# A graph and mixture-of-experts network: VectorE's sum and one-hots are moved ahead of the block's own messages

## The chip, the cores and the metric

One core of a Trainium2 chip runs the whole kernel. The metric is the time of one execution in microseconds; the kernel before took 3406.29 us, the median of three runs (3405.17 to 3412.83).

## The reference, cut to what matters

Four layers are added one after the other to x (128 tiles of 128 nodes, 128 features each): a graph layer with a dense adjacency, a mixture of 4 experts that is gated by a graph attention over 524,288 edges, a dense graph attention, and a mixture of 8 experts. The change lies in the edges' attention of the second layer:

```python
a_src = (h * att_src).sum(-1)
a_dst = (h * att_dst).sum(-1)
e = jax.nn.leaky_relu(a_src[src] + a_dst[dst], negative_slope=0.2)
e_max = jax.ops.segment_max(e, dst, num_segments=M)
ee = jnp.exp(e - e_max[dst])
denom = jax.ops.segment_sum(ee, dst, num_segments=M)
alpha = ee / (denom[dst] + 1e-16)
msg = h[src] * alpha[:, :, None]
agg = jax.ops.segment_sum(msg, dst, num_segments=M).reshape(M, HEADS * NUM_EXPERTS) + b_gat
```

## The kernel before, in words

The kernel is several programs behind each other. The first ones sort the edges by destination, compute the first layer and build a table of the nodes. The last program, `layers`, holds the edges' attention, the experts and the dense attention, interleaved by hand. Edges are taken in 128 blocks, one for each 128 destination nodes; a block has nine chunks of 128 edges (`GC` is 9, padding included).

For a block b these steps follow each other across the engines:

- SyncE loads the block's window of sorted destinations, broadcast over all partitions (`window`, L1670), which waits for `oh_ready` of the block two before; further row and hub windows are queued behind it. GpSimd gathers the source nodes' rows, nine indirect DMAs a block (L1750), into a ring of four; it waits for `msg_ready` of the block that held the slot, and for counts of the experts' matmuls.
- VectorE (DVE) makes two one-hots (`hots`, L2083 and L2086): which edge goes to which node, for the sum, and its transpose, for the look-up. It signals `oh_ready`.
- TensorE (PE) looks up the destination's part of the score for each edge (`look_up`, L1762, nine matmuls) and signals `look_done`.
- DVE makes the messages (`messages`, L1084 to L1091, six operations that wait for each other) once `look_done` and `gathered` allow, and signals `msg_ready`.
- PE sums the messages by destination (`attend`, L1771, nine matmuls into one bank) and signals `sum_done`; right behind it, it does the look-up of block b + 1.
- DVE adds the sum to its accumulator (`add_sum`, L1095 and L1097) in the attend of block b + 1.

One-hots, messages and PSUM banks are doubled: block b uses number b % 2.

The order of the work is written out by hand: each engine goes through turns `i`, and a turn has four attends (blocks 4i + 2 to 4i + 5), called first to fourth here. Between them stand the steps of the experts of a group of four tiles and of the dense attention of two later stages. On PE, an expert is an up-projection (L1786, a record of four matmuls) and a down-projection (L1795, sixteen). On DVE, `expert` adds its result to x (L2181). Behind the second attend DVE adds biases, makes norms (L2206 to L2220) and the scaled x of L2216, for which PE waits at L1879 (`turn_x2`). ScalarE (ACT) does the GELUs (L1940), copies out of PSUM (L1957 the turned gates, L1999 the projection h) and counts (L2028). Its copy at L1999 is what DVE waits for at L2228.

In the first turns (i < 1) DVE also makes one-hots of the remaining edges (L2107), which PE counts (L1815), and in the turns before i = 4 there are no experts of the last layer yet.

Of the kernel before, what the change touches and what calls it, by code (L numbers as in the profile page):

```python
# [31 lines left out]
GC = 9  # L32
GROUP = GC * P
RING = 4
# [1040 lines left out]
def high_halves(split):  # L1075

    return split.bitcast(BF16).rearrange("p c a (f t) -> p c a f t", t=2)[:, :, :, :, 1]


def messages(v, me, looked, got, look, split):  # L1080

    high = high_halves(split)
    msg, left, last = (split[:, :, a, :] for a in range(PARTS))
    me.link(v.tensor_reduce(look[:, :, :], looked.rearrange("p (c a h) -> p c h a", c=GC, a=PARTS), AX.X, ALU.add))  # L1084
    me.link(v.tensor_tensor(look[:, :, :], look[:, :, :], got[:, :, HC + HEADS:TAB], ALU.mult))
    me.link(v.tensor_tensor(msg[:, :, HC:ROW], look[:, :, :], got[:, :, HC:HC + HEADS], ALU.max))
    me.link(v.tensor_tensor(msg[:, :, 0:HC].rearrange("p c (h f) -> p c h f", f=CH),  # L1087
                            got[:, :, 0:HC].rearrange("p c (h f) -> p c h f", f=CH),
                            over(msg[:, :, HC:ROW].unsqueeze(3), [P, GC, HEADS, CH]), ALU.mult))
    me.link(v.tensor_tensor(left, msg, high[:, :, 0, :], ALU.subtract))  # L1090
    return v.tensor_tensor(last, left, high[:, :, 1, :], ALU.subtract)  # L1091
# [403 lines left out]
def layers(nc, adj, sorted_src, sorted_dst, rest_sums, first, table, made, w, keep, out):  # L1495
# [20 lines left out]
    LOOK = PARTS * HEADS  # L1516
# [7 lines left out]
    with Scope(nc, "lay") as s:  # L1524
        ident, iota_b, node_no, least, base_no = (keep[n] for n in ("ident", "iota_b", "node_no", "least", "base_no"))
        idx, to, wide, hub_wide = (keep[n] for n in ("idx", "to", "wide", "hub_wide"))
        node_col, halves, got = (keep[n] for n in ("node_col", "halves", "got"))
# [8 lines left out]
        look = s.sb("look", [P, GC, HEADS])  # L1536
        split = s.sb("split", [P, 2, GC, PARTS, ROW])
# [50 lines left out]
        b_att = [s.bank(f"b_att{k}") for k in range(2)]  # L1588
# [7 lines left out]
        wide_in, hub_in, rows_in, gathered = (keep[n] for n in ("wide_in", "hub_windows_in", "rows_in", "gathered"))  # L1596
# [3 lines left out]
        look_done = s.sem("look_done")  # L1600
        msg_ready = s.sem("msg_ready")
# [54 lines left out]
        def has_block(b):  # L1656
            return 0 <= b < tiles
# [408 lines left out]
        def _(v):  # L2066
            edge, pick, dense, add = (Done(v, sem) for sem in own)
# [14 lines left out]
            def hots(b):  # L2082
                v.tensor_tensor(oh[:, b % 2, :, :], node_col[:, :, :], over(low[:, b, :].unsqueeze(1), [P, P, GC]),  # L2083
                                ALU.is_equal)
                v.wait_ge(wide_in[b % 2], 16 * (b // 2) + 16)
                v.tensor_scalar(oht[:, b % 2, :], wide[:, b % 2, :], node_no[:, b:b + 1], None, ALU.is_equal)\  # L2086
                    .then_inc(oh_ready, 1)

            def attend(b):
                if has_block(b):  # L2090
                    v.wait_ge(look_done, b + 1)
                    v.wait_ge(gathered[b % RING], (16 * GC) * (b // RING + 1))
                    messages(v, edge, b_att[b % 2][:, 0:GC * LOOK], got[:, b % RING, :, :], look,
                             split[:, b % 2, :, :, :]).then_inc(msg_ready, 1)
                if has_block(b - 1):
                    v.wait_ge(sum_done, b)
                    edge.mark(add_sum(v, edge, b_att[(b - 1) % 2][:, GC * LOOK:GC * LOOK + SUM], added,
                                      acc[:, b - 1:b, :]))
                if b >= 0 and has_block(b + 1):
                    hots(b + 1)  # L2100

            def rest_hots_of(n):

# [186 lines left out]
            for i in range(-1, LAST):  # L2290
                b, m, t, f = 4 * i + 2, i - QUAD, i - QUAD - 1, i - QUAD - 2
# [147 lines left out]
```

## Time and profile before

| what | value |
|---|---|
| median of three runs | 3406.29 us |
| the profiled execution's own time | 3408.03 us |
| its span | 3406.0 us |
| PE busy | 75% of the span |
| DVE busy | 72% |
| ACT busy | 52% |
| GpSimd (POOL) busy | 34% |
| mean granted clock of PE | 0.867 of full speed |

The span is the time from the first to the last instruction on the core; the execution's own time has some 2 us around it. A matmul's record has a modelled end. The granted clock of PE has two levels, 1.00 (2.4 GHz) and 0.50 (1.2 GHz). Idle time is shown in brackets behind an instruction, with what ended it, as far as the profile could tell; "issue" and "remote" stand where no instruction could be named.

### The profile page before, as it was taken

What the parts mean: (1) busy time and instruction counts of PE and PEld (TensorE: products, weight loads), DVE (VectorE), ACT (ScalarE), POOL (GpSimd) and SP (SyncE); (2) the same over time, 40 slices, a digit from 0 to 9 for tenths busy, and PEclk for the clock granted to TensorE, in tenths of its full rate; (3) what the DMA queues carried; (4) which work ended last, traced back from release to release, by engine and by line L of the source; (5) the groups of instructions that cost most, each with busy time, mean ns of one, the idle gap of its engine ahead of it and who ended that gap; (6) DMA issues with size and microseconds to landing.
All of it is one profiled execution on the core that took longest, in us unless ns stands there. A gap on an engine that the chain in (4) does not pass through costs nothing.

```text
span 3406.0 us, 48930 instructions
## 1 busy us (share of the span) xinstructions
PE 2558.5 (75%) x15405; PEld 1894.7 (56%) x15406; DVE 2451.7 (72%) x7195; ACT 1765.8 (52%) x3180; POOL 1157.5 (34%) x1205
## 2 busy tenths in 40 slices
PE   1789888988888832115878788788888888788889
PEld 0566666666656622014656565556656656556666
DVE  7888888878778645237667776876777777686774
ACT  0566666666666612014555555555455555555654
POOL 0000000000000027655656555555655656556200
PEclk9999999999999965556888888888888888888899
DMA  2011111111111033223232332323323232232300
GB/s 91 32 50 50 47 53 44 53 41 38 50 38 44 32 100 86 38 55 89 63 84 66 71 87 62 85 70 78 76 63 92 66 85 66 62 93 66 82 13 10
DMA packets 228554, 210.48 MB, mean 62 GB/s; under 512 B 70780, under 2 KB 160584, under 8 KB 227656
## 3 DMA queue, kind: packets, MB, share of 16 engines
q1 hardware_dynamic: 190152, 190.84, 18.8%
q0 software_dynamic: 37280, 14.38, 4.7%
q8 instruction: 123, 2.02, 0.2%
q10 hardware_dynamic: 864, 2.14, 0.2%
q14 instruction: 135, 1.11, 0.1%
HBM read 159.49 MB, written 47.74 MB: 61 GB/s over the span
## 4 chain that ended last, share of the span: by engine, by line
DVE 22%; PE 19%; another core or an unknown queue 9%; issue 9%; ACT 2%; POOL 2%; DVEq 0%; DMA 0%; ACTq 0%; POOLq 0%
PE lay_b_y L1795 8%; PE lay_b_z L1786 7%; DVE keep_x L2181 6%; POOL keep_got L1750 2%; PE lay_b_b L1837 1%; DVE lay_oht L2086 1%; PE lay_b_att L1762 1%; DVE lay_split L1090 1%; DVE lay_oh L2083 1%; DVE lay_split L1091 1%; DVE lay_stats L2206 1%; PE lay_b_g L1887 1%; DVE lay_split L1087 1%; ACT lay_unused L2028 1%
## 5 line engine op out<-in xcount | busy, mean ns | idle before, releaser
L1750 POOL DMA_INDIRECT keep_got<-node_table,keep_idx x1143 | 1122.1, 982 | 772.5 <-issue 304.9
L1795 PEld LDWEIGHTS lay_b_y<-lay_w,lay_hid 128*128 128x128 f32 x4096 | 542.2, 206 | 164.5 <-issue 162.6
L1786 PE MATMUL lay_b_z<-lay_xin,lay_w 128*128 128x512 f32 x1024 | 581.3, 696 | 11.6 <-ACT lay_hid L1940 7.7
L1795 PE MATMUL lay_b_y<-lay_w,lay_hid 128*128 128x128 f32 x4096 | 551.9, 290 | 38.5 <-issue 34.9
L2181 DVE SCALAR_TENSOR_TENSOR keep_x<-lay_b_y,lay_gates,keep_x 128x128 f32<-128x128 f32 x1024 | 288.0, 344 | 373.4 <-remote 204.4
L1940 ACT ACTIVATE lay_hid<-lay_b_z,lay_b 128x512 f32<-128x512 f32 x512 | 330.3, 682 | 405.6 <-PE lay_b_z L1786 207.1
L899 POOL MEMSET find_ones<- 128x128 f32 x1 | 0.2, 204 | 1203.5 <-POOLq L49 1203.5
L2028 ACT ACTIVATE lay_unused<-keep_hub_wide,keep_halves 128x1152 bf16<-128x1152 uint16 x256 | 320.3, 1251 | 138.1 <-DMA keep_hub_wide<-sorted_dst 68.5
L1786 PEld LDWEIGHTS lay_b_z<-lay_xin,lay_w 128*128 128x128 f32 x1024 | 201.1, 218 | 176.8 <-issue 154.2
L472 PE MATMUL front_b_h<-front_xt,front_m 128*128 128x512 f32 x512 | 256.8, 628 | 41.1 <-ACT front_act_m L582 33.8
L225 DVE TENSOR_TENSOR sort_keys<-sort_keys 128x1024 f32<-128x1024 f32 (+2 forms) x182 | 257.5, 1415 | 32.1 <-ACT sort_keys L550 29.1
L226 DVE TENSOR_TENSOR sort_keys<-sort_keys 128x1024 f32<-128x1024 f32 (+2 forms) x182 | 256.9, 1412 | 0.0
L428 PE MATMUL front_b_h<-front_w,front_agg_t 128*128 128x512 f32 x256 | 140.1, 674 | 94.2 <-DVE front_hb L716 71.9
L1771 PE MATMUL lay_b_att<-lay_split,lay_oh 128*128 128x60 bf16 x1152 | 90.9, 229 | 158.5 <-DVE lay_split L1091 112.2
L582 ACT ACTIVATE front_act_m<-front_b_h,front_mb 128x512 f32<-128x512 f32 x256 | 170.3, 684 | 64.9 <-PE front_b_h L472 64.5
L491 PEld LDWEIGHTS front_b_turn<-front_m,front_act_m 128*128 128x128 f32 x1536 | 184.2, 192 | 31.1 <-issue 31.1
L491 PE MATMUL front_b_turn<-front_m,front_act_m 128*128 128x128 f32 x1536 | 187.0, 275 | 0.0
L1771 PEld LDWEIGHTS lay_b_att<-lay_split,lay_oh 128*128 128x128 bf16 x1152 | 84.2, 156 | 176.7 <-DVE lay_split L1091 122.3
L472 PEld LDWEIGHTS front_b_h<-front_xt,front_m 128*128 128x128 f32 x512 | 89.0, 195 | 156.4 <-ACT front_act_m L582 100.4
L437 PE MATMUL front_b_ht<-front_diag,front_hb 128*128 128x128 f32 x1024 | 131.6, 282 | 35.0 <-ACT front_diag L573 22.7
L437 PEld LDWEIGHTS front_b_ht<-front_diag,front_hb 128*128 128x128 f32 x1024 | 120.5, 193 | 47.5 <-issue 29.2
L2181 DVE SCALAR_TENSOR_TENSOR keep_x<-lay_y,lay_gates,keep_x 128x128 f32<-128x128 f32 x512 | 145.7, 346 | 0.7
(397 smaller groups left out, 4244.0 us busy)
## 6 DMA issues: line engine op xcount, KB each, us to landing
keep_wide<-sorted_dst SPq DMA_DIRECT2D x128, 288.0 KB
keep_hub_wide<-sorted_dst SPq DMA_DIRECT2D x128, 288.0 KB
made<-front_y SPq DMA_DIRECT2D x128, 256.0 KB, 2.0
lay_y<-made SPq DMA_DIRECT2D x32, 1024.0 KB
keep_got<-node_table,keep_idx POOLq DMA_INDIRECT x1152
front_adj<-in_adj SPq DMA_DIRECT2D x32, 256.0 KB, 3.1
keep_x<-in_x SPq DMA_DIRECT2D x32, 256.0 KB, 3.5
lay_adj<-in_adj SPq DMA_DIRECT2D x32, 256.0 KB
```

The lines of the kernel that those rows point to most:

```text
L225: me.mark(v.tensor_tensor(o[:, :, 0, :], s[:, :, 0, :], s[:, :, 1, :], ALU.min))
L226: return v.tensor_tensor(o[:, :, 1, :], s[:, :, 0, :], s[:, :, 1, :], ALU.max)
L437: mm = pe.matmul(b_ht[c % 2][:, P * j:P * j + P], hb[:, j, P * c:P * c + P], diag[:, j, :], start=True, stop=True)
L472: pe.matmul(b_h[c][:, :], m1[:, e, P * c:P * c + P], flat(xt[:, :, :]), start=True, stop=True)\
L491: mm = pe.matmul(bank[:, P * j:P * j + P], act_m[n % 2][:, c, P * j:P * j + P], m2[:, e * MK + c, :], start=(c == 0), stop=(c == MK - 1))
L1750: pool.indirect_dma_start(out=got[:, b % RING, c, :], out_offset=None, in_=table, in_offset=bass.IndirectOffsetOnAxis(ap=idx[:, b % AHEAD, ...
L1771: mm = pe.matmul(b_att[b % 2][:, GC * LOOK:GC * LOOK + SUM], oh[:, b % 2, :, c], high_halves(split[:, b % 2, :, :, :])[:, c, :, :] .rearra ...
L1786: pe.matmul(b_z[c][:, :], w1[:, e, P * c:P * c + P], flat(xin[g % 2][:, :, :]), start=True, stop=True).then_inc(z_done, 1)
L1795: mm = pe.matmul(b_y[n % 2][:, P * j:P * j + P], hid[n % 2][:, c, P * j:P * j + P], w2[:, e * HK + c, :], start=(c == 0), stop=(c == HK - 1))
L1940: act.activation(hid[n % 2][:, c, :], b_z[c][:, :], ACT.Gelu, bias=b1[:, e * HK + c:e * HK + c + 1]).then_inc(hid_ready, 1)
L2028: act.activation(unused[:, :], hub_wide[:, b % 2, :], ACT.Sign, bias=halves[:, u, b:b + 1], accum_out=signs[:, u, b:b + 1]).then_inc(count ...
L2181: ins = v.scalar_tensor_tensor(out=here, in0=made_here[:, P * j:P * j + P], scalar=gates[n][:, g * TB + j, e:e + 1], in1=here, op0=ALU.mul ...
```

## The change

In DVE's `attend(b)` of the last program, the adding of block b - 1's sum and the one-hots of block b + 1 are put ahead of block b's messages. PE's, GpSimd's, SyncE's and ACT's orders stay.

```diff
             def attend(b):
-                if has_block(b):
-                    v.wait_ge(look_done, b + 1)
-                    v.wait_ge(gathered[b % RING], (16 * GC) * (b // RING + 1))
-                    messages(v, edge, b_att[b % 2][:, 0:GC * LOOK], got[:, b % RING, :, :], look,
-                             split[:, b % 2, :, :, :]).then_inc(msg_ready, 1)
                 if has_block(b - 1):
                     v.wait_ge(sum_done, b)
                     edge.mark(add_sum(v, edge, b_att[(b - 1) % 2][:, GC * LOOK:GC * LOOK + SUM], added,
                                       acc[:, b - 1:b, :]))
                 if b >= 0 and has_block(b + 1):
                     hots(b + 1)
+                if has_block(b):
+                    v.wait_ge(look_done, b + 1)
+                    v.wait_ge(gathered[b % RING], (16 * GC) * (b // RING + 1))
+                    messages(v, edge, b_att[b % 2][:, 0:GC * LOOK], got[:, b % RING, :, :], look,
+                             split[:, b % 2, :, :, :]).then_inc(msg_ready, 1)
```

## Rows read from the trace of the kernel before

**Rows 1.** Windows: stretch, its us, busy us (count) of PE, PEld, DVE, ACT, POOL, PEclk.

```profile
1290.00:1612.00 322.00, 84.73 (x666) 66.41 (x666) 164.01 (x493) 73.54 (x129) 207.45 (x202) 0.52 0.31 69
1612.00:3220.00 1608.00, 1310.41 (x7830) 963.55 (x7831) 1173.98 (x4269) 877.90 (x1517) 917.43 (x945) 0.86 0.32 75
```

**Rows 2.** Timeline of one first attend: start us, us, engine, line, operation, idle before.

```profile
2433.76 0.27 DVE L1084 TENSOR_REDUCE lay_look<-lay_b_att 128x36 f32<-128x108 f32 x1
...
2435.25 0.35 DVE L1091 TENSOR_TENSOR lay_split<-lay_split 128x180 f32<-128x180 f32 x1
...
2435.65 0.75 PE L1771 MATMUL lay_b_att<-lay_split,lay_oh 128*128 128x60 bf16 x9 [1.04 <-DVE lay_split L1091]
...
2436.64 0.51 DVE L2086 TENSOR_SCALAR lay_oht<-keep_wide,keep_node_no 128x1152 bf16<-128x1152 uint16 x1
...
2437.21 0.71 PE L1762 MATMUL lay_b_att<-keep_far_parts,lay_oht 128*128 128x12 bf16 x9 [0.81 <-DVE lay_oht L2086]
```

**Rows 3.** Waits of the steady part, 1612 to 3220: total us, times, longest.

```profile
PE lay_b_att L1762 <- DVE lay_oht L2086: 20.3, 25, 0.8
...
PE lay_b_att L1762 <- issue: 18.0, 25, 1.2
```

**Rows 4.** Timeline behind the second attend of that turn, and L1879 of another turn.

```profile
2446.74 0.51 DVE L2086 TENSOR_SCALAR lay_oht<-keep_wide,keep_node_no 128x1152 bf16<-128x1152 uint16 x1
...
2447.31 0.70 PE L1762 MATMUL lay_b_att<-keep_far_parts,lay_oht 128*128 128x12 bf16 x9 [0.38 <-issue]
...
2447.88 1.96 PE L1786 MATMUL lay_b_z<-lay_xin,lay_w 128*128 128x512 f32 x4
...
2451.46 0.60 PE L1829 MATMUL lay_b_b<-keep_ident,lay_gates 128*8 128x128 f32 x4
...
2452.99 0.59 ACT L1957 ACTIVATE lay_gate_t<-lay_b_b 8x512 f32<-8x512 f32 x1 [1.90 <-PE lay_b_b L1829]
...
2453.99 1.11 DVE L2216 TENSOR_SCALAR lay_xn<-keep_x,lay_mv,lay_rstd 128x128 f32<-128x128 f32 x4
...
2455.16 0.66 PE L1879 MATMUL lay_b_g<-keep_ident,lay_xn 128*128 128x128 f32 x4 [1.38 <-issue]
...
2994.43 0.66 PE L1879 MATMUL lay_b_g<-keep_ident,lay_xn 128*128 128x128 f32 x4 [0.57 <-DVE lay_xn L2216]
```

**Rows 5.** Timeline of the third attend of the same turn.

```profile
2460.22 0.52 DVE L2086 TENSOR_SCALAR lay_oht<-keep_wide,keep_node_no 128x1152 bf16<-128x1152 uint16 x1
...
2462.62 0.67 PE L1771 MATMUL lay_b_att<-lay_split,lay_oh 128*128 128x60 bf16 x9
...
2463.13 0.68 PE L1762 MATMUL lay_b_att<-keep_far_parts,lay_oht 128*128 128x12 bf16 x9
```

**Rows 6.** Timeline of DVE at the start of the last program: its waits.

```profile
1366.71 0.27 DVE L1084 TENSOR_REDUCE lay_look<-lay_b_att 128x36 f32<-128x108 f32 x1 [4.86 <-DMA keep_got<-node_table,keep_idx]
...
1436.69 0.27 DVE L1084 TENSOR_REDUCE lay_look<-lay_b_att 128x36 f32<-128x108 f32 x1 [10.37 <-remote]
...
1490.19 0.27 DVE L1084 TENSOR_REDUCE lay_look<-lay_b_att 128x36 f32<-128x108 f32 x1 [16.51 <-issue]
...
1529.32 0.69 DVE L2228 TENSOR_TENSOR lay_lg<-lay_h,lay_a 128x512 f32<-128x512 f32 x1 [10.76 <-issue]
...
1548.19 0.27 DVE L1084 TENSOR_REDUCE lay_look<-lay_b_att 128x36 f32<-128x108 f32 x1 [5.89 <-issue]
```

**Rows 7.** PE by windows of 8 us from L1879 (busy, PEclk), and an up-projection.

```profile
1671.50:1679.50 8.00, 6.71 (x44) 1.00 0.37 84
1734.50:1742.50 8.00, 7.46 (x39) 0.79 0.37 84
...
2439.85 3.78 PE L1786 MATMUL lay_b_z<-lay_xin,lay_w 128*128 128x512 f32 x4
```

**Rows 8.** Timeline of a gather behind its wait, and of a window load's issue.

```profile
2435.86 0.94 POOL L1750 DMA_INDIRECT keep_got<-node_table,keep_idx  x1 [1.70 <-DVE lay_split L1091]
...
2447.41 0.33 SPq L1670 DMA_DIRECT2D keep_wide<-sorted_dst  x1
```

## The prediction, made before the changed kernel was run

> **What bounds the kernel now.** I read the windows of the stages first, then the timeline of one turn of the last program, then DVE's waits at its start. The last program has a slow start of 322 us in which PE is busy 84.7 us, and a steady part of 1608 us in which PE is busy 1310 and DVE 1174 [rows 1]. In the steady part neither is the bound alone: each turn (four blocks, eight experts; 1608 us over 27 turns, 59.6 us) hands the work to and fro. Only these two stretches hold an `attend`, so nothing before 1290 us and after 3220 us can change, apart from its place in time.
>
> One attend of DVE runs from 2433.76 to 2437.15: the messages to 2435.60 (1.84 us), then sum and one-hots to 2437.15 (1.55 us). PE starts its sum matmuls 0.05 us after the messages end, waits again, and starts the look-up 0.06 us after the one-hots end; it is through at 2437.92 [rows 2]. The list of waits counts 50 such waits ahead of the look-up in the steady part, 38.3 us in all, so 0.77 each [rows 3]: in about half of its 108 attends PE is early, in the others DVE is.
>
> **The change part by part.** It adds, removes and resizes no instruction: six message operations, two of the sum and two of the one-hots stay, 3.39 us an attend. What moves is the signal `msg_ready`, 1.55 us later behind a start of DVE that waits for nothing, and `oh_ready`, 1.84 us earlier.
>
> *PE at an attend where it is early.* It now waits once, for the messages, which end where the one-hots ended (2437.15). Then sum and look-up follow each other: the look-up starts 0.51 us behind the sum's start in an attend without a wait [rows 5]. It ends at 2437.15 + 0.06 + 0.51 + 0.71 = 2438.43, against 2437.92: **0.51 us later**. That is so 50 times [rows 3], in the first and second attend of a turn. What takes it up: in the first attend, PE's wait for the same DVE in the second one. In the second, the wait at L1879 for `x2_ready`. DVE goes from the end of its one-hots (2447.25) to L2216 (2455.10) on its own, and PE had waited 1.38 us there [rows 4]. L1879 stands with such a wait in all 26 turns whose windows I compared; 1.38 is the usual value, the smallest is 0.57, in a turn where PE came late to its attends and so loses nothing. So 50 x 0.51 = 25.5 us of delay are shown and I put **0** of them on the path; if that cover were gone, the second attend alone would cost 27 x 0.51 = 13.8 us.
>
> *Third and fourth attends.* DVE's one-hots end at 2460.74 and PE begins its sum at 2462.62, without idle time [rows 5]. The messages now end at 2460.74: still 1.88 us ahead. Cost 0; if PE were as early as in the first attends, 0.51 each.
>
> *Start of the last program.* Here DVE waits ahead of the messages: 4.86 us for the gathered rows (the last of five such waits, at 1366.71), then 10.37, 16.51 and 5.89 us, and another of their kind at 1515, between the last two [rows 6]. The one-hots and the sum now lie inside these waits. From the end of such a wait to the end of the attend DVE takes 1.84 instead of 3.39, and is 1.55 us ahead. PE's look-up, which the next wait hangs on, begins 1.84 + 0.06 + 0.51 = 2.41 behind the wait's end instead of 3.45: 1.04 ahead. The five waits for gathers are paced by GpSimd, so only the last one's gain goes on: 1.0. Of the four long waits I count 1.04 each for those at 1436.69 and 1490.19 and 1.55 for that at 1548.19 (PE comes late there, and the 0.51 is not added); the one at 1515 is followed by a wait of 10.76 us at L2228 for ScalarE, which takes its gain. Sum 1.0 + 1.04 + 1.04 + 1.55 = **4.6 us gained**. Bounds: 0, if what ends those waits isn't moved by PE's earlier look-up; 9 x 1.55 = 14 us if all nine count in full. I take 4.6, nearest to what the order of the rows lets through.
>
> *Queues.* GpSimd waits for `msg_ready` of the block four back (1.70 us ahead of the gather at 2435.86) [rows 8]; it starts up to 1.55 us later. The rows it fetches are used by the attend four blocks on, a turn of 59.6 us later, so 0. In the start its five blocks of gathers have no wait for DVE. Were that ring the bound, it would be 1.55 a block. SyncE issues its window load 0.16 us after the one-hots end (2447.41) [rows 8]; it may issue 1.84 us sooner, with its next row and hub loads behind it: more lead for loads that nobody waits for in the steady part, 0. DVE's wait for `sum_done` now stands at the head of the attend; PE made that sum an attend before (through at 2436.40 [rows 2], while the next attend of DVE ends at 2447.25 and so begins near 2443.9), so 0; behind it are queued only the one-hots and messages that waited there anyway.
>
> *The clock.* PE's up-projection of four matmul records took 3.78 us at the granted clock of 1.2 GHz and 1.96 at 2.4 [rows 7, 4]. In 9 of the 26 stretches of 8 us from L1879 on, the granted clock was 0.79 on average, as in the stretch at 1734.5, and in the others 1.00, as at 1671.5: 0.21 x 8 / 0.5 makes 3.4 us at 1.2 GHz, which follow the wait of 1.38 us there and cost PE 1.7 us of work. The change shortens exactly this wait, to some 0.87 us, and lengthens those at the first two attends. I enter 0, and keep 9 x 1.7 = 15 us of gain for the range.
>
> **Sum.** 0 + 0 - 4.6 + 0 = -4.6 us. The profiled execution took 3408.03 us (span 3406.0), 1.7 above the median of 3406.29, so it would come to 3403.4, and the median to **3401.7 us**. A measurement of this kernel tells 0.2% (6.8 us) from no change.
>
> **Rivals.**
> 1. *PE's clock stays up behind L1879.* For: each drop of the kind counted above follows that idle time [rows 7], and half or more of nine could vanish at 1.7 us each: 7.7 more, 3394 us. Against: the same idle time appears at the attends. Chance 0.28.
> 2. *Slower: the cover at L1879 isn't real.* Place: L1879, once a turn. Price 0.51 x 27 = 13.8, less 4.6: +9.2, 3415.5 us. It decides where PE's true slack is under 0.51 us. For it: ScalarE begins to copy the turned gates at 2452.99, 0.93 us after PE's record of them ended (2451.46 + 0.60) [rows 4], though it had been idle 1.90 us: PE may run behind its records. Against: 1.38 - 0.93 leaves 0.45, just below 0.51, so at most a tenth of a us a turn would pass by that row. The Trainium skill, Perfetto Trace Analysis, Tensor Engine Instruction, says that the profiler estimates a matmul's end and doesn't observe it. By that rule, the row's 0.93 us is what the record leaves out. Chance 0.12.
> 3. *Slower: the clock falls at the second attend.* PE's idle pieces there (0.38 us at 2447.31 [rows 4], 0.77 in the mean) become a single one ahead of the sum. If PE ran at 1.2 GHz for 3.4 us behind it, it would lose 1.7 us, of which 0.87 are covered: 0.8 a turn, 22 us if in all 27, about 3424; with a third of the turns 3409. Against: the up-projection behind that attend (2447.88) took 1.96 us, at full clock. The Trainium skill, TensorE: Matmul & The Clock Gate, Part 1, says that idling throttles the array and activity releases it. By that rule, a longer single pause is worse than two short ones, and the sum would be +3 to +18 in place of -4.6. The trace agrees only at L1879. Chance 0.06.
> 4. *It changes nothing that lasts.* The long waits at the start end when they did before, and all later waits take the rest: 3406.3 us. For: the three long ones shown have a releaser that the view calls "issue" or "remote", not a named instruction [rows 6]. Chance 0.12.
>
> **How the numbers follow.** Forecast 0.42 (3401.7; its own range 3396 to 3406, as the start's gain runs from 0 to 10). Faster by over 0.2% is under 3399.5: rival 1 whole, and a third of the forecast's case: 0.28 + 0.14 = 0.42. Slower is over 3413.1: rival 2 and most of 3, 0.12 + 0.04 = 0.16. The rest, 0.42, is within 0.2%. The range goes down to rival 1 with most of its nine drops gone (3401.7 - 14 = 3388) and up to rival 2 (3415).
>
> **What would show it.** PE's wait ahead of L1762 gone in the first attends, that ahead of L1771 there near 2.6 us instead of 1.04; the wait at L1879 near 0.87; the long waits of DVE now ahead of the same L1084 with L2083 and L2086 inside them; turns of the same length; the last program's first 320 us shorter by 4 to 5. Wrong, if L1879 keeps a wait of 0.87 and the turns still lengthen (then it is GpSimd, the loads or the clock), if L1879's wait falls by more than 0.51, or if the granted clock of the steady part moves from 0.86 by over 0.01.

## The result, and the profile after

The changed kernel took **3418.88 us** (median of 15 runs, 3407.47 to 3428.32); the kernel before took 3401.59 us beside it (15 runs, 3389.99 to 3412.83). The ratio is **1.0054, 95% interval 1.0039 to 1.0069**: slower by 0.54%, 17.3 us between the medians and 18.4 by the ratio. Forecast was 3401.7 us, with a range up to 3415. It started from a median of 3406.29 us of three runs, so as a ratio it was 0.9986.

The profiled execution of the changed kernel has a span of 3412.0 us against 3406.0 before, so the two traces show 6 us of the 17. The window of the last program's steady part, changed kernel (columns as in [rows 1]):

```profile
1612.00:3220.00 1608.00, 1298.78 (x7777) 951.61 (x7778) 1164.17 (x4243) 871.87 (x1511) 918.70 (x941) 0.85 0.31 73
```

Against [rows 1] the steady part does a little less in the same time: 7777 matmul records instead of 7830 and 4243 instructions of DVE instead of 4269. Something has become longer there, on no engine's busy time.

The waits of the steady part, changed kernel (total us, times, longest), which answer to [rows 3]:

```profile
PE lay_b_att L1771 <- DVE lay_split L1091: 60.2, 28, 2.9
...
PE lay_b_g L1879 <- DVE lay_xn L2216: 19.8, 24, 0.9
...
PE lay_b_att L1771 <- issue: 19.6, 22, 1.5
...
PE lay_b_att L1762 <- issue: 1.5, 3, 0.5
```

PE's wait ahead of the look-up (38.3 us in 50 waits before) is down to 1.5 us. The one ahead of the sum has grown from 30.5 us in 36 waits (19.1 us for L1091 and 11.4 under "issue") to 79.8 us in 50. The wait at L1879 is 0.82 us each (19.8 / 24) where it was 1.38. The timeline of the second attend of the same turn as in [rows 4], changed kernel (start us, us, engine, line, operation, idle before):

```profile
2447.57 0.35 DVE L1091 TENSOR_TENSOR lay_split<-lay_split 128x180 f32<-128x180 f32 x1
...
2447.98 0.72 PE L1771 MATMUL lay_b_att<-lay_split,lay_oh 128*128 128x60 bf16 x9 [0.90 <-issue]
...
2448.54 0.69 PE L1762 MATMUL lay_b_att<-keep_far_parts,lay_oht 128*128 128x12 bf16 x9
...
2455.81 0.66 PE L1879 MATMUL lay_b_g<-keep_ident,lay_xn 128*128 128x128 f32 x4 [0.83 <-issue]
```

DVE's attend ends at 2447.92, the look-up at 2449.23: 1.31 us behind, where it was 0.76 (2447.25 to 2448.01 in [rows 4]). That is 0.55 us where the forecast had 0.51, and by the records the wait at L1879 took it up, 1.38 to 0.83. Yet the turns are longer: from one L1879 to the next 59.1 and 60.1 us in turn before, 59.65 and 60.5 after (medians of the turns under 61.2 us, which come in two lengths; some in each trace are 2 to 4 us longer).

**Where in the turn.** I laid the turns of each trace over each other, at L1879. DVE adds the results of the second dense layer's experts to x, four instructions of L2181 an expert; call the last expert's add y7. From y7 to the end of DVE's second attend is one stretch, from there over L1879 to the next y7 the other. Before, they take 16.1 and 44.0 us in the mean of 24 turns; after, 16.05 and 44.4. So the loss lies in the second stretch. In these two traces it appears between L1879 and the add of expert 3, counted from 0 (median of its start behind L1879: 9.95 us before, 10.45 after), and the median of y7 is 0.5 us later too. One turn of each, from the timeline: the adds of experts 0 and 1 beside L1879, expert 3's down-projection on PE, DVE's add of it, and y7. Before the change:

```profile
2455.09 2.38 DVE L2181 SCALAR_TENSOR_TENSOR keep_x<-lay_b_y,lay_gates,keep_x 128x128 f32<-128x128 f32 x8
...
2460.75 2.03 PE L1795 MATMUL lay_b_y<-lay_w,lay_hid 128*128 128x128 f32 x16
...
2465.15 1.13 DVE L2181 SCALAR_TENSOR_TENSOR keep_x<-lay_b_y,lay_gates,keep_x 128x128 f32<-128x128 f32 x4 [2.84 <-remote]
...
2490.71 1.13 DVE L2181 SCALAR_TENSOR_TENSOR keep_x<-lay_b_y,lay_gates,keep_x 128x128 f32<-128x128 f32 x4 [5.12 <-remote]
```

The changed kernel:

```profile
2455.75 2.38 DVE L2181 SCALAR_TENSOR_TENSOR keep_x<-lay_b_y,lay_gates,keep_x 128x128 f32<-128x128 f32 x8
...
2461.40 2.03 PE L1795 MATMUL lay_b_y<-lay_w,lay_hid 128*128 128x128 f32 x16
...
2466.49 1.12 DVE L2181 SCALAR_TENSOR_TENSOR keep_x<-lay_b_y,lay_gates,keep_x 128x128 f32<-128x128 f32 x4 [2.87 <-remote]
...
2492.08 1.13 DVE L2181 SCALAR_TENSOR_TENSOR keep_x<-lay_b_y,lay_gates,keep_x 128x128 f32<-128x128 f32 x4 [5.17 <-remote]
```

From the first row of each, PE's record of the down-projection begins 5.66 us behind before and 5.65 after: by PE's records nothing is late. DVE's add of it starts 10.06 and 10.74 us behind that row, and y7 35.62 and 36.33. The add starts well behind the recorded end of what it waits for: 2462.78 to 2465.15 before (2.37 us), 2463.43 to 2466.49 after (3.06 us), and DVE is idle for all or nearly all of that.

**When PE's signals come.** The trace also holds the time of each semaphore signal, which the rows don't print; I compared the signals of PE with the recorded ends of the matmuls that send them. In the kernel before, all 1050 that could be matched before 1296 us and after 3188 us come within 0.1 us of that end. Between these times 636 of 938 come later, in the turn shown by some 7 us at most: the look-up of the second attend ends at 2448.02 and signals at 2449.76, that of the third ends at 2463.81 and signals at 2470.86. They come in bursts. Behind the fourth attend of this turn the look-up signals at 2489.61, the two halves of an up-projection at 2490.32 and 2490.36, a down-projection at 2490.52 and L1863 at 2490.58. PE has no record of work between L1863 and 2491.25, while ScalarE waits for that signal:

```profile
2486.30 0.66 PE L1863 MATMUL lay_b_g<-keep_ident,lay_att 128*128 128x128 f32 x4
...
2490.60 0.60 ACT L1963 ACTIVATE lay_att_t<-lay_b_g 128x512 f32<-128x512 f32 x1 [4.24 <-remote]
```

The two halves of an up-projection are never under 0.85 us apart in the records of the steady part, but 92 of the 380 spacings between their signals there are under 0.1 us. Work that is recorded as 0.85 us can't have been done in 0.1, so in these bursts the signals are held and let go together, and the array had done most of the work before. PE isn't undisturbed there either: behind the third attend of this turn single matmuls of L1847 start 0.7 us apart (2468.67, 2469.37, 2470.09). The late signals have a place, too: GpSimd's gathers run from 1296.7 to 3188.0 us, and the matmuls whose signals are late end from 1310.6 to 3187.3. In all other traces of kernels that take about 3400 us the last matmul with a late signal likewise ends at most 1.5 us behind the last gather.

### The profile page after: what moved, and what is told of

Its sections match the earlier page's. It is cut to its first block, busy times and chain, and to the rows that moved or that the text cites. A ratio compares the mean times of both kernels' runs of the same rounds, so it can differ in the third digit from the quotient of the medians.

```text
span 3412.0 us, 49046 instructions
## 1 busy us (share of the span) xinstructions
PE 2554.6 (75%) x15405; PEld 1889.9 (55%) x15406; DVE 2447.9 (72%) x7195; ACT 1763.8 (52%) x3180; POOL 1161.8 (34%) x1205
## 4 chain that ended last, share of the span: by engine, by line
DVE 28%; PE 13%; another core or an unknown queue 10%; issue 7%; POOL 1%; ACT 1%; DVEq 1%; DMA 0%; ACTq 0%; POOLq 0%
DVE keep_x L2181 8%; PE lay_b_y L1795 5%; PE lay_b_z L1786 5%; DVE lay_oh L2083 2%; POOL keep_got L1750 1%; DVE lay_oht L2086 1%; DVE lay_stats L2206 1%; DVE lay_split L1090 1%; DVE lay_split L1087 1%; PE lay_b_b L1837 1%; DVE lay_split L1086 1%; DVE lay_look L1085 1%; DVE lay_look L1084 1%; DVE lay_lg L2236 1%
## 5 line engine op out<-in xcount | busy, mean ns | idle before, releaser
L2181 DVE SCALAR_TENSOR_TENSOR keep_x<-lay_b_y,lay_gates,keep_x 128x128 f32<-128x128 f32 x1024 | 287.7, 343 | 398.4 <-remote 293.5
L491 PEld LDWEIGHTS front_b_turn<-front_m,front_act_m 128*128 128x128 f32 x1536 | 184.2, 192 | 31.1 <-issue 31.1
L2181 DVE SCALAR_TENSOR_TENSOR keep_x<-lay_y,lay_gates,keep_x 128x128 f32<-128x128 f32 x512 | 145.3, 345 | 1.3 <-issue 0.5
```

Of the source, the lines that this page charges most:

```text
L491: mm = pe.matmul(bank[:, P * j:P * j + P], act_m[n % 2][:, c, P * j:P * j + P], m2[:, e * MK + c, :], start=(c == 0), stop=(c == MK - 1))
L2181: ins = v.scalar_tensor_tensor(out=here, in0=made_here[:, P * j:P * j + P], scalar=gates[n][:, g * TB + j, e:e + 1], in1=here, op0=ALU.mul ...
```

## The experiments

Three theories were tested. **A**, as the expectations have it: PE's array is behind what its records show, so at L1879 no slack exists, and the second attend's look-up, 0.51 us later, delays all up to y7. (By the signals told above it is rather PE's signals that are behind; the experiments below don't tell the two apart.) **B**: the third attend does it. **C**: the messages that come later in every attend do it. All times are medians; each ratio is to runs of the kernel before beside it, with its 95% interval. In most kernels with a condition VectorE also waits once more (`edge.wait()`) ahead of an add of a sum that would follow other edge work directly; that wait wasn't measured by itself.

### The new order in all but the second attend, and in it alone

```
                behind = b % 4 != 3      # first run: own messages last, but not in 4i + 3
                behind = b % 4 == 3      # second run: only there
                if not behind:
                    own_messages()
...
                if behind:
                    own_messages()
```

> The new order in the first, third and fourth attends of a turn, the old order in the second attend (block 4i + 3). Theory A, TensorE runs a backlog: when the change puts the second attend's look-up 0.51 us later, everything up to the third attend comes 0.51 us later, because TensorE still works on what stands in its queue when the transposes of L1879 are recorded as waiting. Then only the second attend costs anything: turns are back at 59.1 and 60.1 us (59.65 and 60.5 with the change), the start keeps its gain of 4 us, and the time is 3397 us, ratio 0.9987. Theory B, the third attend costs it: in the medians of the turns the 0.5 us appear between L1879 and the third expert's add, and there messages are 1.5 to 2 us later in a turn. Then this kernel is as the changed one: turns 59.65 and 60.5, 3419 us, ratio 1.005. Theory C, the messages that come 1.25 us later hold back GpSimd's gathers in all four attends alike: most of the loss stays, 3414 us, ratio 1.0035.

Measured: 3394.82 us, **0.9975 (0.9959 to 0.9990)**.

> The reverse: the old order everywhere but in the second attend of each turn. Theory A: the whole loss and none or little of the gain at the start: 26 to 28 turns of 0.5 us, +13 to +14 us, turns at 59.65 and 60.5, 3415 us, ratio 1.004. Theory B: as before, 3402 us, ratio 1.000, turns at 59.1 and 60.1. Theory C: a quarter of the loss, +4 us, ratio 1.001.

Measured: 3419.79 us, **1.0048 (1.0029 to 1.0066)**.

The whole loss sits in the second attend, and the rest of the change is a gain, larger than A said (0.9987). B is out, and so is C as a loss in every attend alike. The last pair of runs repeats the second kernel on another chip: 1.0037 (1.0023 to 1.0051).

### The new order in the start alone

```
                behind = b < 4 * (QUAD + 2) + 2
```

> The new order only for the blocks below 18, before the experts of the two dense layers run beside the blocks; the old order from there. Theories A and B: the start's gain of 4.0 to 4.6 us stays and nothing is given back: 3397 us, ratio 0.9987, turns at 59.1 and 60.1. A rival, that the 4 us of lead are given back whatever the order behind (the work stands in another phase to transfers and clock): 3402 us or more, with turns longer than before's.

Measured: 3401.43 us, 1.0000 (0.9980 to 1.0021). The start's gain of 4.6 us is neither shown nor excluded. The traces say why: from the first L2086 of the last program to the fourth L1879 it is 437.2 us before and 434.7 after, and 429.3 in this run, but 423.7, 428.8 and 429.1 in the three runs with a doubled look-up below, which have the old order there. Executions differ by more than the gain.

### PE makes the look-up ahead of the sum

```
             def attend(b):
+                if b >= 0 and has_block(b + 1):
+                    look_up(b + 1)
                 if has_block(b):
                     pe.wait_ge(msg_ready, b + 1)
...
-                if b >= 0 and has_block(b + 1):
-                    look_up(b + 1)
```

> As the changed kernel, but TensorE's attend makes the look-up of the next block ahead of the sum of this one, so that behind the messages only the sum is left (0.5 us less of matmuls behind VectorE's last instruction of attend). Theory A: the second attend is through about as early as before the change: turns at 59.1 and 60.1, with the gain at the start 3397 us, ratio 0.9987. Theory B or C, where the lateness of messages itself is what costs: 3419 us, ratio 1.005, turns at 59.65 and 60.5.

Measured: 3395.23 us, **0.9980 (0.9965 to 0.9995)**. VectorE's order is that of the changed kernel, and GpSimd's waits for the messages (L1091) in the steady part are no shorter: 28.9 us before the change, 84.0 in the changed kernel, 94.0 here. Only PE has less to do behind the messages, and the ratio is 0.998 where the changed kernel had 1.0054. It is the clearest sign against C, and it agrees with A in that the time hangs on what PE does behind the messages.

### One more look-up's worth of PE work, at three places

```
-                for c in range(GC):
+                for c in list(range(GC)) * (2 if b % 4 == 0 and b > 0 else 1):
```

(0 is the look-up made in the second attend, 3 in the first, 1 in the third; VectorE as before the change.)

> The kernel before, VectorE's order untouched; TensorE makes the nine matmuls of the look-up in the second attend of a turn twice (0.54 us more of its work right there, nothing later on VectorE). Theory A, TensorE has a real backlog from there to the third attend although 1.38 us of waiting are recorded at L1879: each turn is 0.5 us longer, 59.65 and 60.5, 28 times: +14 us, 3417 us, ratio 1.004. Rival: the recorded wait of 1.38 us is real slack of TensorE and the loss of the change came from VectorE's and GpSimd's side, through messages that come 1.25 us later: nothing is longer, 3403 us, ratio 1.000, and the wait at L1879 falls to 0.84.

Measured: 3407.80 us, 1.0016 (0.9998 to 1.0033).

> The same doubling in the first attend of a turn. Behind it TensorE waits for the second attend's messages (0.58 to 1.05 us recorded), and VectorE's own order sets when they come: in theory A the 0.54 us go into that wait and nothing is longer, 3403 us, ratio 1.000. Should TensorE be late from the first attend on already, +14 us, ratio 1.004.

Measured: 3405.63 us, 1.0014 (0.9995 to 1.0033).

> The same doubling in the third attend of a turn, where TensorE is late for its messages by microseconds. Theory A says TensorE works without a pause from the second attend's look-up to the seventh expert, so 0.54 us of work cost the same here: +14 us, ratio 1.004. That VectorE's later messages cost nothing there and TensorE's own work does would show which of the two the third attend hangs on. Rival, slack in each attend: ratio 1.000.

Measured: 3409.26 us, 1.0019 (1.0001 to 1.0037).

A missed here: 1.004 was expected at the second and third attend and 1.000 at the first, and the three places can't be told apart. At both of them 1.004 lies outside the interval. A record of the doubled look-up, and the waits at L1879 of that run:

```profile
2442.29 1.24 PE L1762 MATMUL lay_b_att<-keep_far_parts,lay_oht 128*128 128x12 bf16 x18 [0.79 <-DVE lay_oht L2086]
```
```profile
PE lay_b_g L1879 <- DVE lay_xn L2216: 15.4, 18, 0.9
```

The doubling puts the look-up's recorded end 0.54 us later and L1879's wait at 0.86 us (15.4 / 18), just as the change does, for a third of its price. So the recorded end isn't what the turn hangs on, and a fixed backlog of work on PE isn't either. One reading is that nine small matmuls behind nine others cost less than they show, and that the change costs more because PE gets nothing to do until the messages are there; no run tests it.

### Two more orders for VectorE

Own messages last but ahead of the add of the sum behind, PE's look-up first (the look-ups in the other bank, since PE and VectorE may then be at work at the same time):

```
-                    mm = pe.matmul(b_att[b % 2][:, LOOK * c:LOOK * c + LOOK],
+                    mm = pe.matmul(b_att[(b + 1) % 2][:, LOOK * c:LOOK * c + LOOK],
...
             def attend(b):          # VectorE's
                 if has_block(b - 1):
                     v.wait_ge(sum_done, b)
-                    edge.mark(add_sum(v, edge, b_att[(b - 1) % 2][:, GC * LOOK:GC * LOOK + SUM], added,
-                                      acc[:, b - 1:b, :]))
                 if b >= 0 and has_block(b + 1):
                     hots(b + 1)
                 if has_block(b):
...
-                    messages(v, edge, b_att[b % 2][:, 0:GC * LOOK], got[:, b % RING, :, :], look,
+                    messages(v, edge, b_att[(b + 1) % 2][:, 0:GC * LOOK], got[:, b % RING, :, :], look,
...
+                if has_block(b - 1):
+                    edge.mark(add_sum(v, edge, b_att[(b - 1) % 2][:, GC * LOOK:GC * LOOK + SUM], added,
+                                      acc[:, b - 1:b, :]))
```

(against the changed kernel, and PE's attend as in the fourth run; what the other bank does by itself wasn't measured, here or in the kernels below)

> VectorE in every attend: the next block's one-hots, then the block's own messages, then the sum of the block behind; TensorE: look-up of the next block, then the sum. The look-ups lie in the other one of the two banks. TensorE is through with the second attend about 0.6 us earlier than before the change, measured from VectorE's end of attend (only the sum stands behind the messages, and the add of the sum behind stands after them). Theory A: turns get shorter by up to 0.6 us, until VectorE's chain to x2_ready binds: between 3383 us (0.6 us for 28 turns, ratio 0.995) and 3399 us (ratio 0.9985) if there is no slack left to win. Rival, TensorE's end of the second attend does not matter and the messages 1.0 us later do: slower than before, 3410 us, ratio 1.002.

Measured: 3400.99 us, 0.9987 (0.9970 to 1.0005). That can't be told from the kernel before, and it excludes the 1.002 of lateness by itself.

Messages first, then the one-hots, then the add of the sum behind (against the kernel before, PE's order as there, the look-ups in the other bank as above):

```
...
                 if has_block(b - 1):
                     v.wait_ge(sum_done, b)
-                    edge.mark(add_sum(v, edge, b_att[(b - 1) % 2][:, GC * LOOK:GC * LOOK + SUM], added,
-                                      acc[:, b - 1:b, :]))
                 if b >= 0 and has_block(b + 1):
                     hots(b + 1)
+                if has_block(b - 1):
+                    edge.mark(add_sum(v, edge, b_att[(b - 1) % 2][:, GC * LOOK:GC * LOOK + SUM], added,
+                                      acc[:, b - 1:b, :]))
```

> The old order with one exchange: VectorE makes a block's own messages first, then the one-hots of the next block, then the add of the sum behind (the look-ups lie in the other bank, so that the add and the look-up are in different banks). Messages come as early as before the change; the look-up's input comes 0.46 us earlier than before at VectorE's unchanged end of attend, where the change had the look-up end 0.51 us later. Theory A, the turn hangs on when TensorE is through with the second attend's look-up: turns 0.46 us shorter, 28 times: 3391 us, ratio 0.996; or as before, 3404 us, if the next thing binds at once. Rival, the loss came from the lateness of the messages: 3404 us, ratio 1.000.

Measured: 3390.90 us, **0.9967 (0.9951 to 0.9983)**.

The fourth run's kernel, with the look-ups in the other bank, and with the add of the sum behind after the messages where `b % 4 == 3`, ahead of the one-hots elsewhere:

> The changed kernel with TensorE's look-up ahead of the sum (as in the fourth run), and in the second attend of a turn the add of the sum behind after the messages (as in the eighth run), the look-ups in the other bank. It joins what was fastest: 3396 us was the new order with look-up first, and the second attend is through 0.5 us earlier still. Theory A: 3388 us, ratio 0.9955, if TensorE's end of the second attend still binds; 3396 us, ratio 0.998, if that is used up.

Measured: 3389.62 us, **0.9959 (0.9939 to 0.9979)**: the fastest by ratio in the lagging condition, and faster than both kernels (0.9979 at most, against 1.0000 at least for the changed one in its two measurements). In the prompt condition, told below, it wasn't tried.

### The other attends by themselves

```
                behind = b % 4 < 2      # third and fourth attend
                behind = b % 4 == 2     # first attend
```

> The new order in the third and fourth attends alone. Theory A has them at 0 in the steady part, where TensorE is late for them by microseconds; with half of the gain at the start: 3402 us, ratio 0.9995. The kernel with the new order in all but the second attend gained 8.5 us, though, and the one with it at the start alone 1.3 us: if the rest of 7 us comes from here (sums and one-hots out of VectorE's way before TensorE's signals come), 3397 us, ratio 0.998.

Measured: 3391.67 us, **0.9971 (0.9952 to 0.9990)**.

> The new order in the first attend alone. Theory A: TensorE's 0.51 us go into the wait of the second attend: 0 in the steady part, with a quarter of the gain at the start 3403 us, ratio 0.9997. Rival, the first attend loses as the second does, +14 us, ratio 1.004. If the 7 us that the run with all but the second attend gained beside the start come from here, 3397 us, ratio 0.998.

Measured: 3401.19 us, 0.9996 (0.9975 to 1.0017).

So the parts are: first attend 0 within 0.2%, third and fourth -0.29%, second +0.37 to +0.48%, measured on three chips. They add up to +0.1 to +0.2%, if parts from different chips may be added.

### Four runs in another condition

For the next four kernels the hardware was in another condition: there the kernel before takes **3125.22 us** (31 runs, 3114.60 to 3138.42) in place of 3402 or so, under the same chip number as the four kernels before these, though that may not be the same piece of hardware. I call it the prompt condition, and that of all other runs the lagging one; the reason for the names is below. The edits: the order just told where `b % 4 == 3` alone; that order in the first and second attend joined with the change's order in the third and fourth (where the add now also waits for the block's own look-up, so it is not a plain sum of the two); and the change's order under these conditions:

```
                behind = b % 4 == 0                                    # third attend alone
                behind = b % 4 < 2 and b >= 4 * (QUAD + 2) + 2         # third and fourth, from block 18 on
```

> As the run with one-hots ahead of the add of the sum behind (-0.33% in every attend), but in the second attend of a turn alone; the others in the old order. Theory A: the look-up of the second attend comes through 0.34 us earlier in the records (0.42 instead of 0.76 us behind VectorE's end of attend), 28 times: -9.5 us, ratio 0.997. Rival, the gain of that run came from the third and fourth attends: ratio 1.000.

Measured: 3140.14 us, **1.0047 (1.0030 to 1.0065)**.

> First and second attends: messages, one-hots, add of the sum behind (-0.33% when in all four). Third and fourth: the change's order (-0.29% alone). If the two gains have different places they add up: ratio 0.994, 3382 us. If both come from the third and fourth attends, where either order has the one-hots and the look-up's input earlier: ratio 0.997, 3392 us.

Measured: 3120.29 us, 1.0011 (0.9977 to 1.0045).

> The new order in the third attend alone. If the gain of the third and fourth attends is made in the third, where VectorE reaches the second expert's add 0.45 us earlier (its links no longer stand idle there): ratio 0.997. If it is made in the fourth: 1.000. Half and half: 0.9985.

Measured: 3127.11 us, 1.0005 (0.9990 to 1.0021).

> The new order in the third and fourth attends, from block 18 on alone, where the experts run beside them. If the gain is made in the steady part, 28 turns of 0.35 us: ratio 0.997. If it is made in the start, where the new order as a whole gave 0.9998 +- 0.002: 1.000.

Measured: 3123.76 us, 0.9990 (0.9974 to 1.0006).

The first is slower, the other three can't be told from the kernel before; none repeats the gain of its model. Their traces, though, show what the lagging condition hides. The same places of the timeline as above, in the last of the four runs (its L2190 is L2181, its L2225 is L2216):

```profile
2263.94 2.38 DVE L2190 SCALAR_TENSOR_TENSOR keep_x<-lay_b_y,lay_gates,keep_x 128x128 f32<-128x128 f32 x8
...
2264.00 0.66 PE L1879 MATMUL lay_b_g<-keep_ident,lay_xn 128*128 128x128 f32 x4 [1.38 <-DVE lay_xn L2225]
...
2269.59 2.03 PE L1795 MATMUL lay_b_y<-lay_w,lay_hid 128*128 128x128 f32 x16
...
2271.71 1.13 DVE L2190 SCALAR_TENSOR_TENSOR keep_x<-lay_b_y,lay_gates,keep_x 128x128 f32<-128x128 f32 x4 [0.57 <-PE lay_b_y L1795]
...
2290.71 1.13 DVE L2190 SCALAR_TENSOR_TENSOR keep_x<-lay_b_y,lay_gates,keep_x 128x128 f32<-128x128 f32 x4 [2.91 <-PE lay_b_y L1795]
```

PE's record of the down-projection stands at the same place, 5.65 us behind the first row, and lasts 2.03 us. But DVE starts 0.09 us behind its end (2271.62 to 2271.71), where it took 2.37 us in the lagging condition, and y7 comes 26.77 us behind the first row instead of 35.62. So with the same records PE's results reach the other engines microseconds later in the one than in the other. In the trace of this run, and in those of the other three, no signal of PE comes over 0.1 us late, though the same 1143 gathers run. In the kernel before, the stretch from the second attend to y7 falls from 43.5 us in the turn with L1879 at 3116 to 35.4 in the next, in which the gathers end; in this run the turn in which they end has 34.6. So the lag takes both, the gathers and the condition. A wait at L1879 that both show, 1.38 us in each, can be slack in one alone; the changed kernel wasn't run in the prompt condition, so that it is slack there isn't shown. The groups of the whole kernel say the same (line, engine, operation | busy us, mean ns | idle before it and what ended it), first before the change, then in the prompt condition:

```profile
L2181 DVE SCALAR_TENSOR_TENSOR keep_x<-lay_b_y,lay_gates,keep_x 128x128 f32<-128x128 f32 x1024 | 288.0, 344 | 373.4 <-remote 204.4 <-PE lay_b_y L1795 104.0 <-issue 60.4
```

```profile
L2190 DVE SCALAR_TENSOR_TENSOR keep_x<-lay_b_y,lay_gates,keep_x 128x128 f32<-128x128 f32 x1024 | 287.7, 343 | 184.2 <-PE lay_b_y L1795 176.0 <-issue 1.1 <-DVE keep_x L2190 1.1
```

Where the signals are prompt, almost every wait has PE's name (176.0 of 184.2 us). "Remote" and "issue", 264.8 of 373.4 us, go with the lag.

**The clock behind L1879.** In the prompt condition turns take 50.2 and 52.2 us in turn, or 51.9 and 53.9. The windows of 5 us from an L1879 on (columns as in [rows 1]) tell which. In the last of the four runs, a turn of 53.8 us and one of 52.2:

```profile
1798.20:1803.20 5.00, 4.46 (x21) 4.09 (x22) 4.70 (x17) 1.75 (x5) 2.75 (x4) 0.66 0.42 125
2314.30:2319.30 5.00, 4.46 (x27) 3.29 (x28) 4.70 (x17) 2.48 (x7) 3.78 (x5) 1.00 0.50 124
```

Where the granted clock fell to 1.2 GHz behind PE's wait at L1879, the turn is 1.6 us longer. Of 24 turns this hit 19 in the first of the four runs (3140 us), 11 in the third (3127), 8 in the second (3120) and 5 in the last (3124). The first brings the look-up 0.34 us earlier and so lengthens the wait at L1879 to 1.73 us. At 1.6 us a turn, its 14 such turns more than in the last run are worth 22 us, more than the 16 us between the two; as no trace of the kernel before exists in this condition, that its loss comes from them is argued and not shown. The second has the same wait and only 8 such turns in its profiled execution, so the length of the wait is not all that decides; what else does isn't settled.

### The change again

> The changed kernel itself. On a chip where TensorE's signals come with their recorded ends (the kernel before at 3125 us): the 0.51 us of the second attend's look-up go into the wait at L1879 (1.38 to 0.85 us), no turn is longer for it, and if the shorter wait keeps the clock at full level behind L1879 more turns take 50.2 and 52.2 us instead of 51.9 and 54.0: between ratio 0.990 (none at half level there, 1.65 us for some 15 turns) and 1.000. The rival, that the second attend's order costs 0.5 us a turn on every chip: ratio 1.005. On a chip of the first kind (3402 us): 1.005 again.

Measured: 3409.57 us, **1.0014 (1.0000 to 1.0028)**; before 3404.40.

> The new order in the second attend alone, as in the second run (ratio 1.0048 there). On a chip where signals come with their recorded ends: ratio 0.990 to 1.000 by the clock behind L1879, for the same reason as the changed kernel. Rival: 1.005 on every chip. On a chip of the first kind: 1.005.

Measured: 3419.80 us, **1.0037 (1.0023 to 1.0051)**.

Both met the lagging condition, so what the change does in the prompt one wasn't tried. The loss in the second attend repeats. The change as a whole costs less than in the first measurement, and the two intervals don't meet: +0.14% here, barely clear of nothing, and +0.54% there. The parts told above add up to the former. So its size isn't one number; whether the chip makes the difference isn't known.

### The two stretches of a turn in all these traces

Worked out from the timelines of DVE, 24 turns each, without the last, in which the gathers end; us. "Least" is the shortest of the 24.

| kernel | y7 to end of second attend, mean | from there to y7, mean | least |
|---|---|---|---|
| before | 16.1 | 44.0 | 43.3 |
| changed | 16.05 | 44.4 | 43.8 |
| changed, again | 16.1 | 43.85 | 43.4 |
| only second attend new | 16.1 | 44.5 | 43.3 |
| the same again | 16.1 | 44.1 | 43.3 |
| look-up twice in second attend | 16.1 | 44.5 | 43.4 |
| all but second attend new | 16.1 | 44.0 | 42.9 |
| third and fourth new | 16.1 | 43.8 | 42.8 |
| one-hots ahead of the add | 16.0 | 43.8 | 42.5 |
| prompt condition: third and fourth new in the steady part | 16.1 | 35.6 | 34.6 |

The first column moves by 0.1 us at most. The second holds the waits for PE. In the lagging condition its least value is 43.3 or more in every kernel whose second attend is through later, and 42.5 to 42.9 in the others shown (41.6 to 42.9 with the traces not shown). The profile before the change is the exception: its 43.3 is the same as with only the second attend new. So a floor 0.5 us higher is suggested and not shown. On top lie some 2 us in a part of the turns, scattered from execution to execution, which is why one trace is off by several us.

## Why the prediction was wrong

- **What binds.** Right that DVE's own chain from the second attend to L2216 stays (7.9 to 8.1 us to L1879 in the median of every trace).
- **First and second attends: the failed step.** The delay of 0.51 us was right in size and place: in the turn shown the look-up ends 1.31 us behind the attend, where it was 0.76. That it lasts nowhere, a term of 0, rested on "the wait at L1879 for `x2_ready`", and on its 1.38 us. In the first attend the cover held (0.9996). In the second it didn't: 1.0048 and 1.0037 when that attend alone is new, 0.9975 when it alone is old. The price had been worked out, 13.8 us; 16.3 and 12.6 us (the ratios times 3404, less it) were measured. The wait is on record, but it isn't slack: the signals of the matmuls around it, the second attend's look-up among them, come late, some by microseconds, and ScalarE and DVE wait for those signals and not for the end of PE's wait. That much is shown. How a look-up 0.5 us later becomes half a us or more of a turn through them is argued; as the doubled look-up costs a third, it isn't the 0.5 us of work alone.
- **Third and fourth attends.** Put at 0, since PE is late there. In the lagging condition it was a gain of 0.29%, some 10 us; in the prompt one, from block 18 on, 0.10% (0.26 faster to 0.06 slower), which is within the noise. Why there is one isn't settled.
- **Start.** 4.6 us of gain, neither shown nor excluded (1.0000, 0.9980 to 1.0021). The forecast's whole gain of 4.6 us was this term.
- **Queues.** 0 for later messages is borne out: with the look-up first, messages just as late gave 0.998. But the gathers themselves are not without a part: PE's signals are late only while they run. The prediction had no term for that.
- **The clock.** The steady part's mean went from 0.86 to 0.85. The drops behind L1879 did go, as rival 1 had it, from 9 of 24 turns to none within 5 us of L1879. More time at half clock now lies 10 to 22 us behind it: 2.9 us a turn before, 3.8 after, 4.4 in the changed kernel's second profile, and 5.5 and 5.6 in the two profiles with only the second attend new. So rival 1 had the mechanism and not the gain, and a part of the loss may be the clock's; no run separates it. In the prompt condition such a drop costs 1.6 us a turn.
- **Rival 2** ("the cover at L1879 isn't real") is what happened. It gave 3415.5 us, near the 3418.88 measured, and had a chance of 0.12, by a reading that was too small: 0.93 us between a matmul's record and ScalarE's start [rows 4] was taken as all of PE's lag, which left 0.45 of the 1.38 us. The lag was read from one row, ahead of L1879. Behind it, in the same turn, it is 2.37 us, and the share of "remote" and "issue" in DVE's waits stands in the profile of before. The Trainium skill, Perfetto Trace Analysis, Tensor Engine Instruction, says that a matmul's recorded start is where it begins to fetch its data and that only its end is an estimate. By that rule L1879 began when its record says, and the traces don't speak against it: starts stand alike in both conditions. What comes up to 3.06 us behind the recorded ends in the rows above is the signal, so true starts are no proof of slack either.
- **The sign in the text of what would make it wrong** came true to the letter: L1879 keeps a wait (0.83) and the turns lengthen. Of the three causes named for that case, GpSimd, loads and clock, none is shown as they were meant; GpSimd's gathers and the clock can't be ruled out as parts of it.
- **Open**: what holds PE's signals while the gathers run; by which path the second attend's order costs time; why the first measurement gave +0.54% and the second +0.14%; the gain of the third and fourth attends; why doubled look-ups cost a third of what their records show; what the change does in the prompt condition.

## What to carry to other kernels

A wait in a matmul's record is slack only if the engines behind it start right after its end. Compare, over a whole turn, the recorded end of PE's work with the start of whoever was idle for it; if that lags, or the waits end by "remote" or "issue", PE's signals are late: put no slack of PE into the sum, and give a later signal its full price in the range (here the full price, 13.8 us, was near the 16.3 and 12.6 measured). And steps of a few tenths of a per cent didn't carry from one condition to the other here, so such a step wants a second chip before it is kept.

## What the hardware showed that was not expected

- The same program takes some 3402 or 3125 us. The granted clock of the steady part is 0.86 in one (1612 to 3220 us) and 0.92 in the other (1612 to 2930 us), and DVE's add of expert 3 starts 2.37 or 0.09 us behind the record. Between the trace before the change and the last of the four prompt ones, the stretch from the second attend to y7 is 8.4 us shorter in the mean of 24 turns (202 us), and the start up to the fourth L1879 is 86 us shorter (437.2 to 350.8), with the same instructions but for VectorE's order in the third and fourth attends. What puts the hardware into one condition or the other isn't known.
- In the lagging condition PE's semaphore signals are late only while GpSimd's gathers run: 636 of 938 there, none of 1050 outside, and none in any of the four prompt traces.
- Removing one drop of PE's clock can place another: none within 5 us of L1879 after the change, 9 in 24 turns before, and yet a mean of 0.85 against 0.86.
